# Smaller staging pieces in more buffers, and the second-stage loads reordered over two DMA queues

## The reference, cut to what matters

```python
x = L0_attn_x                                  # (8, 2048, 1024), float32
x = _layernorm(x + _L0_attn_ref(x, w_qkv, w_proj))
x = _layernorm(x + _L0_ffn_ref(x, U1, V1, b1, U2, V2, b2))

# attention: 16 heads of 64, causal
qkv = einsum('btc,oc->bto', x, w_qkv); attn = q @ k^T * 64**-0.5, masked
attn = _custom_softmax(attn); out = attn @ v; return out @ w_proj^T
# ffn, low rank (256) in both halves
P = x @ U1; H = gelu(P @ V1 + b1); Q = H @ U2; return Q @ V2 + b2
```

## Time and profile before

| | |
|---|---|
| time, median of 2 runs | 1771.81 us (1769.04 to 1774.59) |
| the profiled execution's own time | 1772.11 us |
| its span, slowest core (6) | 1770.3 us (all cores 1760.8 to 1770.3) |
| TensorE busy | 1202.7 us (68%) |
| VectorE busy | 716.1 us (40%) |
| ScalarE busy | 650.6 us (37%) |
| moved by DMA | 62.47 MB, mean 35 GB/s |
| mean granted TensorE clock, core 6 | 0.747 of full speed |

### The profile page before, as it was taken

The page is one execution under the profiler, slowest core; times in us unless marked ns, Lnnn a source line. Parts: engine busy times, 40 slices in busy tenths (PEclk is TensorE's granted clock), DMA queues, the critical chain, the costliest instruction groups (busy, mean ns, idle before and its releaser), DMA issues.

```text
span 1770.3 us, 16310 instructions; the slowest of 8 cores (1760.8 to 1770.3 us)
## 1 busy us (share of the span) xinstructions
PE 1202.7 (68%) x4454; PEld 431.5 (24%) x4504; DVE 716.1 (40%) x1139; ACT 650.6 (37%) x690; POOL 19.4 (1%) x46
## 2 busy tenths in 40 slices
PE   0188888787877877767777776766672096398960
PEld 0033333222222212222222222222220032143410
DVE  0057878767777771222222222222221053602048
ACT  3421111000000005555556565666560423464650
POOL 0000000000000000000000000000000000000000
PEclk9998999666767657666666676767665596699975
DMA  6700000000000001000000000000007710000004
GB/s 212 252 11 1 1 1 1 1 1 1 1 1 1 1 0 43 13 20 17 13 13 13 13 13 12 12 13 12 19 1 235 226 49 0 0 1 1 1 1 190
DMA packets 23670, 62.47 MB, mean 35 GB/s; under 512 B 2208, under 2 KB 15520, under 8 KB 18976
## 3 DMA queue, kind: packets, MB, share of 16 engines
q1 hardware_dynamic: 20864, 52.52, 9.0%
q0 software_dynamic: 2720, 8.92, 2.2%
HBM read 44.06 MB, written 8.39 MB: 30 GB/s over the span
## 4 chain that ended last, share of the span: by engine, by line
PE 46%; DVE 24%; ACT 15%; DMA 8%; issue 6%; DVEq 1%; ACTq 0%; PEldq 0%; PEld 0%; SPq 0%; POOL 0%; POOLq 0%
DVE mx_sb L362 13%; PE PS L515 10%; ACT pt L531 6%; PE PS L544 6%; PE PS L414 5%; PE PS L332 4%; PE PS L393 4%; PE PS L849 3%; PE PS L831 3%; PE PS L779 3%; DMA stgB<-wqkT 3%; DVE alo_sb L575 2%; DVE x_f L742 2%; DVE x_f L746 2%; ACT lnw L569 2%
## 5 line engine op out<-in xcount | busy, mean ns | idle before, releaser
L362 DVE TENSOR_REDUCE mx_sb<-PS 128x1 f32<-128x512 f32 (+3 forms) x576 | 359.7, 625 | 99.9 <-PE PS L332 32.0
L531 ACT ACTIVATE pt<-PS 128x1024 bf16<-128x1024 f32 (+7 forms) x384 | 297.3, 774 | 219.3 <-PE PS L515 129.2
L515 PE MATMUL PS<-qs,ks 65*128 65x512 bf16 (+3 forms) x640 | 242.2, 458 | 58.1 <-ACT pt L531 36.0
L332 PE MATMUL PS<-kp,qp 64*128 64x512 bf16 (+3 forms) x640 | 212.0, 413 | 102.1 <-DVE mx_sb L362 93.9
L572 DVE CAST abf_sb<-lnw 1x1024 bf16<-1x1024 f32 x32 | 21.8, 681 | 418.3 <-ACT lnw L569 414.4
L544 PE MATMUL PS<-pt,vT_all 128*65 128x512 bf16 (+3 forms) x640 | 188.5, 414 | 0.0
L393 PE MATMUL PS<-x_bf,wqk_bf 128*128 128x512 bf16 x496 | 130.8, 407 | 83.6 <-ACT wqk_bf L289 72.4
L515 PEld LDWEIGHTS PS<-qs,ks 65*128 65x128 bf16 x640 | 69.1, 113 | 229.1 <-issue 209.3
L425 ACT ACTIVATE vT_all<-PS 128x1024 bf16<-128x1024 f32 x16 | 16.4, 1026 | 294.2 <-PE PS L414 294.2
L332 PEld LDWEIGHTS PS<-kp,qp 64*128 64x128 bf16 x640 | 50.4, 97 | 253.9 <-issue 244.9
L414 PE MATMUL PS<-wv_bf,x_bf 128*128 128x512 bf16 x242 | 105.8, 607 | 3.1 <-issue 1.4
(11 more groups left out here) (84 smaller groups left out, 1075.6 us busy)
## 6 DMA issues: line engine op xcount, KB each, us to landing
stgB<-xT SPq DMA_DIRECT2D x8, 1024.0 KB, 6.1
stgB<-wqkT SPq DMA_DIRECT2D x8, 1024.0 KB, 6.8
x_f<-xT SPq DMA_DIRECT2D x8, 1024.0 KB, 6.9
out<-x_f SPq DMA_DIRECT2D x8, 1024.0 KB, 3.9
stgD<-U SPq DMA_DIRECT2D x5, 1024.0 KB, 6.8
stgD<-V SPq DMA_DIRECT2D x5, 1024.0 KB, 6.0
qs<-qp POOLq DMA_DIRECT2D x17, 256.0 KB, 3.7
ks<-kp POOLq DMA_DIRECT2D x17, 256.0 KB, 3.0
```

The source lines that it names most:

```text
L332: prow=prow, PS=PS: e.matmul(PS[:, lo:lo + w], q_pairs[p2][prow:prow + 64, 128 * i:128 * i + 128], k_pairs[p2][prow:prow + 64, a:a + w], s ...
L362: PS=PS: e.reduce_max(mx_sb[:, xcol:xcol + 1], PS[:, lo:lo + w], axis=AX.X),
L515: cpos=cpos: e.matmul(PS0[:, lo:lo + w], k_stage[hb][:, 128 * j:128 * j + 128], q_stage[qb4][:, cpos:cpos + w], start=True, stop=True),
L531: q0=q0: e.activation(pt[:, cpos - q0:cpos - q0 + span], PS0[:, lo0:lo0 + span], AF.Exp),
```

## The change

Three things are changed, and line numbers shift by up to 22.

1. In the load, the pieces are 128x1024 (512 KiB) in four buffers with four streams, in place of 128x2048 (1 MiB) in two. The order x, wqk, x, wqk stays, now by halves of a chunk.
2. For the projection, `wp` gets four buffers of its own (`stgW`, the fourth is `wpstg`), and its DMAs are issued three `ot` ahead; they come first on SP. `x_f32` is loaded in two streams `xr0`, `xr1`, the first two chunks ahead of the loop and each other chunk two `ot` ahead. The U and V pieces are 512 KiB, twenty of them, in two `stgD` buffers of half the size, and GpSimd issues their DMAs.
3. In the layer norm `sm2` is gone and `sm3` is used in place; every second output DMA is issued by GpSimd.

```diff
--- before.py
+++ after.py
@@ -268,21 +268,23 @@
     mx_sb = alloc(grpQKV, "mx_sb", [128, 8], F32, side="right")
 
     grpB = ExitStack()
-    stgB = [alloc(grpB, f"stgB{i}", [128, 2048], F32, side="right")
-            for i in range(2)]
+    stgB = [alloc(grpB, f"stgB{i}", [128, 1024], F32, side="right")
+            for i in range(4)]
     x_bf = alloc(grpB, "x_bf", [128, NCC * T], BF16, side="right")
     wqk_bf = alloc(grpB, "wqk_bf", [128, NCC * 2048], BF16, side="right")
     wv_bf = alloc(grpB, "wv_bf", [128, NCC * 1024], BF16, side="right")
 
     pieceno = [0]
-
-    def load_cast(dst, dstkey, off, hbm_ap, n, stg,
-                  streams=("ld0", "ld1")):
+    LQ = (("ld0", "sync"), ("ld1", "sync"), ("ld2", "sync"),
+          ("ld3", "sync"))
+
+    def load_cast(dst, dstkey, off, hbm_ap, n, stg, streams=None):
         i = pieceno[0]
         pieceno[0] += 1
-        s = stg[i % 2]
-        skey = ("stg", id(stg), i % 2)
-        stream, qeng = streams[i % 2], "sync"
+        k = i % len(stg)
+        s = stg[k]
+        skey = ("stg", id(stg), k)
+        stream, qeng = LQ[k] if streams is None else streams[k]
         p.dma(stream, qeng,
               lambda e: e.dma_start(out=s[:, 0:n], in_=hbm_ap), writes=[skey])
         p.op("scalar",
@@ -290,14 +292,17 @@
              reads=[skey], writes=[dstkey])
 
     for cc in range(NCC):
-        load_cast(x_bf, ("xbf", cc), cc * T,
-                  i_x[128 * cc:128 * cc + 128, :], T, stgB)
-        load_cast(wqk_bf, ("wqk", cc), cc * 2048,
-                  i_wqk[128 * cc:128 * cc + 128, :], 2048, stgB)
+        for h2 in range(2):
+            load_cast(x_bf, ("xbf", cc), cc * T + 1024 * h2,
+                      i_x[128 * cc:128 * cc + 128,
+                          1024 * h2:1024 * h2 + 1024], 1024, stgB)
+            load_cast(wqk_bf, ("wqk", cc), cc * 2048 + 1024 * h2,
+                      i_wqk[128 * cc:128 * cc + 128,
+                            1024 * h2:1024 * h2 + 1024], 1024, stgB)
     wv3 = i_wv.rearrange("(c p) o -> p c o", p=128)
-    for i in range(4):
-        load_cast(wv_bf, ("wv", i), i * 2048, wv3[:, 2 * i:2 * i + 2, :],
-                  2048, stgB)
+    for i in range(8):
+        load_cast(wv_bf, ("wv", i // 2), i * 1024, wv3[:, i:i + 1, :],
+                  1024, stgB)
 
     PSX = (PS0, PS1)
     PSN = ("P0", "P1")
@@ -637,7 +642,7 @@
     p.dma("wp", "sync", lambda e: e.dma_start(
         out=wpstg[:, :].rearrange("p (c o) -> p c o", c=8),
         in_=wp3[:, :, 0:128]),
-        writes=[("wpstg",)])
+        writes=[("stgW", 3)])
 
     p.barrier()
     grpC.close()
@@ -646,9 +651,8 @@
 
     grpD = ExitStack()
     x_f32 = alloc(grpD, "x_f32", [128, NCC * T], F32)
-    stgD = [alloc(grpD, f"stgD{i}", [128, 2048], F32) for i in range(2)]
+    stgD = [alloc(grpD, f"stgD{i}", [128, 1024], F32) for i in range(2)]
     sm1 = alloc(grpD, "sm1", [1, T], F32)
-    sm2 = alloc(grpD, "sm2", [1, T], F32)
     sm3 = alloc(grpD, "sm3", [1, T], F32)
     rbf = [alloc(grpD, f"rbf{i}", [128, 1024], BF16) for i in range(2)]
     sqbf = [alloc(grpD, f"sqbf{i}", [128, 1024], BF16) for i in range(2)]
@@ -665,26 +669,52 @@
     Q_bf = [alloc(grpE, f"Q_bf{i}", [128, 1024], BF16, side="right")
             for i in range(2)]
 
-    for cc in range(NCC):
-        st = "ld0" if cc % 2 == 0 else "ld1"
+    stgW = [alloc(grpD, f"stgW{i}", [128, 1024], F32) for i in range(3)]
+    stgW.append(wpstg)
+
+    def wp_copy(ot):
+        s = stgW[(ot - 1) % 4]
+        p.op("vector", lambda e, s=s, ot=ot: e.tensor_copy(
+            wp_ot[ot % 2][:, :], s[:, 0:1024]),
+            reads=[("stgW", (ot - 1) % 4)], writes=[("wp", ot % 2)])
+
+    def wp_dma(ot):
+        s = stgW[(ot - 1) % 4]
+        p.dma("wp", "sync", lambda e, s=s, ot=ot: e.dma_start(
+            out=s[:, 0:1024], in_=wp3[:, :, 128 * ot:128 * ot + 128]),
+            writes=[("stgW", (ot - 1) % 4)])
+
+    for ot in range(1, 4):
+        wp_dma(ot)
+
+    def x_dma(cc):
+        st = "xr0" if cc % 2 == 0 else "xr1"
         p.dma(st, "sync", lambda e, cc=cc: e.dma_start(
             out=x_f32[:, cc * T:cc * T + T],
             in_=i_x[128 * cc:128 * cc + 128, :]),
             writes=[("xf", cc)])
+
+    x_dma(0)
+    x_dma(1)
+    LF = (("lf0", "gpsimd"), ("lf1", "gpsimd"))
     u13 = i_u1.rearrange("(c p) r -> p c r", p=128)
-    load_cast(U1_bf, ("U1",), 0, u13[:, :, :], 2048, stgD, ("lf0", "lf1"))
+    for j in range(2):
+        load_cast(U1_bf, ("U1",), j * 1024, u13[:, 4 * j:4 * j + 4, :],
+                  1024, stgD, LF)
     for rt in range(2):
-        for hf in range(2):
-            load_cast(V1_bf[rt], ("V1", rt), hf * 2048,
+        for hf in range(4):
+            load_cast(V1_bf[rt], ("V1", rt), hf * 1024,
                       i_v1[128 * rt:128 * rt + 128,
-                           hf * 2048:hf * 2048 + 2048],
-                      2048, stgD, ("lf0", "lf1"))
+                           hf * 1024:hf * 1024 + 1024],
+                      1024, stgD, LF)
     u23 = i_u2.rearrange("(f p) r -> p f r", p=128)
-    for i in range(4):
-        load_cast(U2_bf, ("U2", i), i * 2048, u23[:, 8 * i:8 * i + 8, :],
-                  2048, stgD, ("lf0", "lf1"))
+    for j in range(8):
+        load_cast(U2_bf, ("U2", j // 2), j * 1024, u23[:, 4 * j:4 * j + 4, :],
+                  1024, stgD, LF)
     v23 = i_v2.rearrange("(r p) o -> p r o", p=128)
-    load_cast(V2_bf, ("V2",), 0, v23[:, :, :], 2048, stgD, ("lf0", "lf1"))
+    for j in range(2):
+        load_cast(V2_bf, ("V2",), j * 1024, v23[:, j:j + 1, :], 1024,
+                  stgD, LF)
 
     def ln_stats_half(ot, th, first, last=False):
         buf = th
@@ -716,19 +746,19 @@
...
-        p.op("scalar", lambda e: e.activation(sm2[:, :], sm1[:, :], AF.Square),
-             reads=[("sm1",)], writes=[("sm2",)])
+        p.op("scalar", lambda e: e.activation(sm3[:, :], sm1[:, :], AF.Square),
+             reads=[("sm1",)], writes=[("sm3",)])
...
@@ -752,24 +782,16 @@
                     O_pairs[cc][:, :], x_f32[:, cc * T:cc * T + T], AF.Copy),
                     reads=[("xf", cc)], writes=[("O", cc)])
 
-    def wp_load(ot):
-        i = pieceno[0]
-        pieceno[0] += 1
-        s = stgD[i % 2]
-        skey = ("stg", id(stgD), i % 2)
-        p.dma("wp", "sync", lambda e, s=s, ot=ot: e.dma_start(
-            out=s[:, 0:1024], in_=wp3[:, :, 128 * ot:128 * ot + 128]),
-            writes=[skey])
-        p.op("vector", lambda e, s=s, ot=ot: e.tensor_copy(
-            wp_ot[ot % 2][:, :], s[:, 0:1024]),
-            reads=[skey], writes=[("wp", ot % 2)])
-
     p.op("vector", lambda e: e.tensor_copy(wp_ot[0][:, :], wpstg[:, :]),
-         reads=[("wpstg",)], writes=[("wp", 0)])
+         reads=[("stgW", 3)], writes=[("wp", 0)])
     prev = None
     for ot in range(NCC):
         if ot + 1 < NCC:
-            wp_load(ot + 1)
+            wp_copy(ot + 1)
+        if ot + 4 < NCC:
+            wp_dma(ot + 4)
+        if ot + 2 < NCC:
+            x_dma(ot + 2)
         for th in range(2):
             lo = 1024 * ((2 * ot + th) % 2)
             o0 = ot * T + 1024 * th
@@ -902,8 +924,8 @@
             ln_stats_half(ot, th, ot == 0, last=(ot == NCC - 1))
     ln_math_bcast_apply(xhat_cast=False)
     for cc in range(NCC):
-        st = "out0" if cc % 2 == 0 else "out1"
-        p.dma(st, "sync", lambda e, cc=cc: e.dma_start(
+        st, qe = ("out0", "sync") if cc % 2 == 0 else ("out1", "gpsimd")
+        p.dma(st, qe, lambda e, cc=cc: e.dma_start(
             out=o_out[128 * cc:128 * cc + 128, :],
             in_=x_f32[:, cc * T:cc * T + T]),
             reads=[("xf", cc)])
```

More of the change, by code:

```diff
@@ L718, in ln_math_bcast_apply @@
              writes=[("sm1",)])
-        p.op("scalar", lambda e: e.activation(sm2[:, :], sm1[:, :], AF.Square),
-             reads=[("sm1",)], writes=[("sm2",)])
+        p.op("scalar", lambda e: e.activation(sm3[:, :], sm1[:, :], AF.Square),
+             reads=[("sm1",)], writes=[("sm3",)])
         p.op("vector", lambda e: e.scalar_tensor_tensor(
-            sm3[:, :], PS1[32:33, :], 1.0 / D, sm2[:, :], ALU.mult,
+            sm3[:, :], PS1[32:33, :], 1.0 / D, sm3[:, :], ALU.mult,
             ALU.subtract),
-            reads=[("P1", 0), ("P1", 1), ("P1", 2), ("P1", 3), ("sm2",)],
+            reads=[("P1", 0), ("P1", 1), ("P1", 2), ("P1", 3), ("sm3",)],
             writes=[("sm3",)])
-        p.op("scalar", lambda e: e.activation(sm2[:, :], sm3[:, :], AF.Ln,
+        p.op("scalar", lambda e: e.activation(sm3[:, :], sm3[:, :], AF.Ln,
                                               bias=cst[0:1, 2:3]),
-             reads=[("sm3",), ("cst",)], writes=[("sm2",)])
-        p.op("scalar", lambda e: e.activation(sm3[:, :], sm2[:, :], AF.Exp,
+             reads=[("sm3",), ("cst",)], writes=[("sm3",)])
+        p.op("scalar", lambda e: e.activation(sm3[:, :], sm3[:, :], AF.Exp,
                                               scale=-0.5),
-             reads=[("sm2",)], writes=[("sm3",)])
```

(1 more changed line is left out.)

## The result

The changed kernel takes 1782.2 us (median of 13 runs) against 1771.4 us (12 runs of the kernel before on the same chip): ratio 1.0058, 95% interval 1.0042 to 1.0074. It is 10 us slower, where 19 us less were forecast. The profiled execution took 1787.2 us, its longest span is core 1's, 1785.6 us.

A forecast was written before the change was run, and what follows sets the result against it. The prediction took TensorE's waits for DMA loads and casts, in the first load and the projection, as the bound. Terms -12 - 5.5 - 2.5 + 1 = -19 us gave 1753 us; own range 1744 to 1763, with rivals 1734 to 1773.

The forecast's parts named there:

- I take -12: First load: four half-size buffers reach x_f32's 282 GB/s, last cast at 80.1 us against 92.3, -12 us.
- I take the bytes: Projection weights: 18.9 MB at 282 GB/s take 67 us; last V2 cast at 1403.5 against 1408.93, -5.5 us.
- the -19 that the best rate gave: First load, best bound: at 320 GB/s the last cast ends at 72.9 us, -19 us.
- the lower bound: First load, worst bound: rate up 10% at most, or no gain with SP's extra issues or shorter rows, 0.
- The rival of fixed landing costs: Both loads: half pieces land hardly sooner than whole ones; load -3.5, projection weights +6.5, total 1773.5 us; chance 0.17.
- the rounds alone: Projection weights without other traffic: ten rounds of 5.2 to 5.9 us, last V2 cast at 1387.5 to 1394.5.
- whole-piece landings: Projection weights, slow end: half pieces land in 6.0 and 6.8 us, round 8.0, last V2 cast at 1415.5, +6.5 us.
- the third rival: Projection weights: GpSimd's issuing bounds, 4.1 us per U piece if time goes by rows; total 1786.5 us; chance 0.07.
- The restart, -2.5 us: Projection after the last V2 cast: only the first square stands before TensorE, since wp 1 is cast early; -2.5 us.
- The end, +1 us: Layer norm's end: last output DMA now issued from GpSimd, between 0 and +3, taken as +1 us.
- Everywhere else nothing changes: Stages q, k, v, attention and feed-forward: unchanged and only shifted in time.
- The reading of the bottleneck: Load and projection: TensorE idles behind the last casts; TensorE's and ScalarE's orders keep the projection stall in both kernels.

The follow-up runs named there:

- e1: Changed kernel with the x and wqkT half pieces read as contiguous 512 KiB blocks, leaving the reference's result: 1768.7 us (0.9995 of the kernel before).
- e4: Kernel before with a third 1 MiB staging buffer for the first load, whole rows as before: 1756.3 us (0.9907).
- e9: Changed kernel run again with nothing edited, giving its second profile: 1783.4 us (1.0069 of the kernel before).
- e6: Changed kernel, first load put back, U and V in ten 1 MiB pieces from GpSimd, three wp buffers: 1766.7 us (0.9952 of the kernel before).
- e7: Changed kernel, first load put back, x_f32 chunks 1 to 7 held until the last V2 cast: 1770.4 us (0.9971 of the kernel before).
- e5: Changed kernel, first load put back, U and V issued by SP and x_f32 by GpSimd: 1778.9 us (1.0040 of the kernel before).
- e3: Changed kernel with the first load put back to two 1 MiB buffers: 1779.4 us (1.0044 of the kernel before).
- e8: Changed kernel, first load put back, 1 MiB U and V pieces, three wp buffers, their casts written behind squares: 1720.3 us (0.9720 of the kernel before).
- e10: Squares-first kernel plus three 1 MiB load buffers, wvT pieces behind first q and k slices, x chunk 0 before wp 1: 1694.0 us (0.9538 of kernel before).
- e2: Kernel before with each 1 MiB first-stage load issued as two DMAs of half the columns into the same buffer: 1775.4 us (1.0012).

## Why the prediction was wrong

Its direction and its range were both missed. Two steps failed, the load's "I take -12" and the weights' "I take the bytes". By its own steps:

**The load, -12 us: wrong, +0.7 to +2.2.** The step that failed is "I take -12, because the x_f32 row is the same data, queue and amount in flight". Data, queue and amount were the same, the shape was not: x_f32 is read by whole 8 KiB rows, the new pieces take 4 KiB out of each. The mechanism that I counted on is real: with contiguous half pieces the load ends 10.4 us sooner than before (e1), most of my 12, and with a third whole buffer 15.7 (e4), between my -12 and the -19 that the best rate gave. The half rows take back 11.1 us, the difference between e1 and the changed kernel. I had "shorter rows" in the lower bound, by length; length alone was not it, the 4 KiB transfers of e1 are as short. Why the half rows are slower is open. The rival of fixed landing costs named this stage too and forecast -3.5; its landing did not shorten, but for another reason (and the round of 7.3 us that it rests on would give some -8, not -3.5).

**The weights, -5.5 us: wrong, +9.0 (T 80.0 against 71.0) and +11.6 in the second profile.** T was to be 68 us and came at 80.0 to 82.6. I had three numbers, the rounds alone (5.2 to 5.9 us each), the bytes at full rate (67 us) and whole-piece landings (8.0 us a round), and "I take the bytes". That took the larger of two bounds where the stretch has both in turn: while x travels, a round is long because the queue is shared (V landings of 8.0 us, q0 getting 4.72 of 12.3 MB), and when x is through, the rounds alone can't use the DMAs (154 GB/s, a round of 6.1 us in the U rows above). The rounds alone were priced a little low as well, since GpSimd begins its issue 0.56 us after a cast, where I had 0.2 for handing over. Neither makes up for the other. The slow end, ten rounds of 8.0, is the T that came, but by luck: its own landings of 6.0 and 6.8 give a mean round of 7.7, and the rounds that came are a mix of long ones in company and short ones alone. e6 and e7 show it from both sides: with 1 MiB pieces, twice the amount in flight, T is 66.8, the bytes' number; with the company away it is 70.6. e5 shows that T doesn't fall when SP issues, so the third rival had the place (a slow U and V loop) but the wrong size: GpSimd costs up to 0.8 us a round more than SP, and a U issue of 512 rows took 0.75 us, not 4.1, against 0.53 for 128 rows.
The sentence of the Trainium skill under "Issuing engines are not separate DMA queues" (DMA: Bandwidth & Descriptors) held in e5, by T. The Trainium skill, same page, "Queues, rings and completion order", says that a DMA engine goes round between the queues that have work for it; the trace agrees in so far as q0 got 4.72 MB beside 7.58 on q1, so the queue that TensorE waited for had no precedence. I had used the first rule for bytes only, and not for who gets them. The advice of the Trainium skill, same page, "Measured", to use pieces of 1 MiB or more, which I carried as a rival with 0.17, was the better guide for this stage, as e6 against e3 shows; e1's 296 GB/s with pieces of 512 KiB shows that it isn't the size by itself.

**The restart, -2.5 us: right in its size.** The first square starts 0.1 us before the computed end of the last cast, not 2.8 after it (means). The stall was not removed, as said, and the projection behind the square kept its 64 us.

**The end, +1 us: right**, 1.3 to 1.5 from the layer norm's start on, and behind the last issue as said. In e3, e5 to e8 and e10, which have the same last part, it is 0.8 to 1.2.

**Everywhere else nothing changes: right**, once the clock of one execution is set aside (e9).

**The reading of the bottleneck: right, but not used far enough.** I wrote that TensorE's and ScalarE's orders keep the stall, and took it as given. e8 against e6 shows what that order cost: 46 us from barrier to layer norm. (Of the "first 32 matmuls from 76.47 us" the row shows 25; the others ran before. It changes no term.)

Summed by stages, +0.7 + 3.0 + 5.9 + 1.3 = 10.9 us in the first profile, against a difference of the mean spans of 11.2; 3.0 of it is the clock of that execution, and the second profile has it in the load and in T instead.

## What to carry to other kernels

When a load is cut into smaller pieces, cut it so that each piece is contiguous in memory; a DMA share that rises at an unchanged GB/s is the sign that it was cut the wrong way. A ring of staging buffers must hold enough in flight for its share of the DMAs while others load, and a stretch that is shared at first and alone later has to be priced in both halves. And before loads are made faster, look at who waits for them: here the casts of weights that were not needed for another 120 us stood ahead of the one square that TensorE needed, and moving them (46 us) was worth more than every edit of the loads (15.7 at best, e4).

## What the runs showed of the hardware that I had not expected

- Reading 4 KiB out of every 8 KiB of a 1 MiB block, with four such pieces in flight on each of eight cores, gives 247 GB/s at a DMA share of 0.93; contiguous blocks in transfers of the same length give 296 GB/s at 0.93 (core 1). With two buffers in the kernel before it costs 4.9 us on the 16 MiB read so (e2). At a low rate it isn't seen: the V pieces, most of them 4 KiB out of rows of 16 KiB, land in 4.3 us in e7, the U pieces in 4.4. Why it is slower is open; no run changed the row pitch.
- A 1 MiB DMA lands in 6 to 7 us with two in flight, 7.5 to 7.8 with three (e4, at 317 GB/s), 10.5 to 11.3 beside another queue's 1 MiB transfers (e6, 274 GB/s): the landing time alone says nothing about the rate.
- GpSimd's issue of a staging DMA grows far less than its rows: 0.51 us for 64, 0.53 for 128, 0.75 for 512, 0.88 to 0.93 for 1024 (e6). It begins 0.56 us after the cast that it waits for, SP's 0.07 (e5).
